# Renumbering the slots of the expert rows, and scattering the second half's rows without copies

## The chip, the cores and the metric

The kernel runs on one core of one Trainium2 chip. The metric is device time of one execution in microseconds, from runs of the kernel with the same inputs. A timed figure is the median of several runs; a profile is taken of one further execution. TensorE's clock has two levels, 1.2 and 2.4 GHz, which the profile gives as a granted clock of 0.50 and 1.00.

## What is computed

Two gated layers on x of 64 sequences, 128 tokens each, width 128, with a context of 77 rows per sequence. Each layer is cross attention, then a feed-forward part, both added to x through a tanh gate:

```python
x = x + tanh(g_xattn[0]) * xattn0(layernorm(x), ctx)      # 8 heads of 64
x = x + tanh(g_ffn[0])   * moe(layernorm(x))              # 16 experts, the best 2 of each token
x = x + tanh(g_xattn[1]) * xattn1(layernorm(x), ctx, ctx) # 16 heads of 8
x = x + tanh(g_ffn[1])   * fp8_gemm(layernorm(x))
```

The change lies in the second line, whose core is

```python
vals, idx = top_k(logits, 2)
w = softmax(vals)
h = relu(x @ W1[e] + b1[e]);  y_e = h @ W2[e] + b2[e]     # 128 -> 256 -> 128
out = sum over the two chosen experts of w * y_e
```

## The kernel before

The kernel has three stages, each a pipeline over blocks of 128 tokens (one sequence) or over expert tiles of 128 rows. All five engines run programs of their own that meet on semaphores.

*Stage A* (`step_a`, 64 blocks, some 0 to 465 us): first cross attention, layer norm, gate logits. VectorE picks the two experts of each token along the way. The normed tokens stay in `XN` ("moe_in").

*Routing* (`route(c)`): the tokens are taken in two halves (c = 0, 1) of 32 blocks. When a half has its picks, TensorE counts and VectorE computes in one chain of instructions, each waiting for the one before (`link`), the slot of every token in a list sorted by expert, each expert's part padded to full tiles of 128. The slots go to `POS[k]`, one column per block and k = 0, 1 for the two picks (line 998). The chain ends with the table of experts per tile (line 1014), for which TensorE waits. Routing 0 runs in the middle of stage A, at 260 to 271 us, routing 1 at its end, at 467 to 478 us.

*Scatter*: GpSimd writes the rows of each block to their slots in a DRAM buffer `xs_dram[c]` by two indirect transfers, one for each pick. For half 0 this happens inside stage A; for half 1 in a loop of its own, right after routing 1, while stage B works on half 0. `scatter` (lines 514 to 525) copies the block's rows and its two columns of slots to small buffers first, waits for those copies, and then issues. A semaphore holds it to two blocks in flight.

*Stage B* (`step_b`, 160 tiles, 80 a half, some 480 to 707 us): each tile is transposed (line 1340), multiplied by W1, gets its bias on VectorE, is transposed again (line 1326), goes through relu on ScalarE, is multiplied by W2 and gets the second bias. SyncE loads four tiles at a time (`load_group`, 20 groups a half, two buffers) and stores four results at a time (`store_group`). Before the first load of a half it waits for all scatters of that half (`scattered(c)`); what stands behind in its queue, stores of the half before among it, waits too. A load also waits until the tiles that were in its buffer are transposed (`xsT_mm`), which puts load g after 4(g - 1) transposes.

*After the scatters* GpSimd waits for all of them, prepares constants of stage C (lines 579 to 595) and gathers results: 48 early gathers during the second half of stage B, each paced by the count of transposes, the rest in stage C. A gather takes its indices straight from `POS[k][:, b:b + 1]` and writes into `XN`.

*Stage C* (`step_c`, 64 blocks with 17 steps of lag, some 707 to 1150 us): the two gathered rows are weighted and added, then second cross attention, the fp8 product and the store.

## Time and profile before

| | |
|---|---|
| median of 3 runs | 1159.11 us (1157.23 to 1159.70) |
| the profiled execution's own time | 1153.63 us |
| its span, first to last instruction | 1151.9 us |
| mean granted clock of TensorE | 0.952 |
| busy in the span | TensorE 1035.9 us, VectorE 814.5, GpSimd 650.7, ScalarE 590.3 |
| stage A with routing 1 | 0 to 479.8 us |
| stage B, half 0 / half 1 | first transposes at 479.8 / 598.8 us |
| last transpose of stage B | 700.2 us |

The profile gives busy time by engine, the span in 40 slices of 28.8 us with the granted clock, then the waits: which engine's instruction stood idle until which other instruction or transfer was done. A wait that is long in total costs nothing where its engine isn't the one that everything waits for. The order of reading is: which engine is busy, in which slices it isn't, what it waits for there, and what that in turn waited for. Lines with an index number are single instructions in order of time.

### The profile page before, as it was taken

Reading aid. Unit: us, or ns where it says so; the run is one execution under the profiler, and the core shown is the slowest. Engines: PE = TensorE matmul, PEld = TensorE weight load, DVE = VectorE, ACT = ScalarE, POOL = GpSimd, SP = SyncE. Lnnn points to the kernel's source line nnn. Section 1 sums busy time; section 2 is a strip of 40 time slices with the busy share of each in tenths; the row PEclk is TensorE's granted clock in tenths of the full one; section 3 lists DMA queues with packets and bytes.
Section 4 is the critical chain, followed back from the end, with each engine's and each line's share of the span. In section 5 each row is a group of like instructions: output and inputs, shape, how many; then the busy total and the mean of one; then the engine's idle time right before and its main releaser. Section 6 shows DMA issues by size and latency. Waiting matters only on the chain. (4 is left out here: it accounts for less than half of the span.)

```text
span 1151.9 us, 40516 instructions
## 1 busy us (share of the span) xinstructions
PE 1035.9 (90%) x13498; PEld 844.1 (73%) x13498; DVE 814.5 (71%) x2572; ACT 590.3 (51%) x1415; POOL 650.7 (56%) x1155
## 2 busy tenths in 40 slices
PE   4999999996999997499949996888999999899993
PEld 3787878774777775288848985666788888788882
DVE  1777777776777775655525555577899999799984
ACT  2666666662666564144515442234556555465554
POOL 1333333232777777566663545447777777577656
PEclk9999999997999999599979998799999999899997
DMA  3412112331334300144424543111111111111101
GB/s 76 90 42 52 42 38 61 91 75 40 92 95 108 98 25 27 55 139 140 134 74 130 144 137 89 30 30 29 32 38 37 32 37 38 30 37 34 33 24 31
DMA packets 106902, 74.39 MB, mean 65 GB/s; under 512 B 21360, under 2 KB 98288, under 8 KB 106736
## 3 DMA queue, kind: packets, MB, share of 16 engines
q1 hardware_dynamic: 98544, 55.40, 18.5%
q0 software_dynamic: 8192, 16.79, 4.9%
q8 instruction: 102, 1.67, 0.6%
q14 instruction: 64, 0.52, 0.2%
HBM read 38.60 MB, written 33.55 MB: 63 GB/s over the span
## 5 line engine op out<-in xcount | busy, mean ns | idle before, releaser
L678 ACT ACTIVATE arena<-PS 77x512 f32<-77x512 f32 (+4 forms) x736 | 303.9, 439 | 424.7 <-PE PS L1194 288.4
L1194 PE MATMUL PS<-arena 128*32 128x128 f32 (+5 forms) x9488 | 452.0, 292 | 36.6 <-DMA logit_bias<-in_bias 12.7
L1194 PEld LDWEIGHTS PS<-arena 128*32 128x32 f32 (+4 forms) x9488 | 352.5, 147 | 114.4 <-ACT arena L678 29.1
L604 POOL DMA_INDIRECT moe_in<-moe_results,slot x128 | 130.5, 1020 | 129.1 <-PE PS L1194 63.0
L1194 PE MATMUL PS<-w,arena 128*128 x960 | 192.4, 319 | 2.2 <-ACT arena L741 1.2
L524 POOL DMA_INDIRECT moe_rows<-arena x128 | 127.5, 996 | 71.8 <-POOL arena L520 50.3
L539 POOL TENSOR_TENSOR arena<-arena,minus_half 128x2 f32<-128x2 f32 (+1 forms) x70 | 47.5, 679 | 187.9 <-DVE arena L852 165.8
L1194 PEld LDWEIGHTS PS<-w,arena 128*128 128x128 f32 x960 | 135.0, 195 | 19.3 <-issue 6.2
L1075 DVE TENSOR_TENSOR arena<-PS,b_rows 128x256 f32<-128x256 f32 x160 | 67.7, 424 | 72.1 <-PE PS L1194 50.1
L1194 PEld LDWEIGHTS PS<-arena,wk_wq 128*128 128x128 f32 x512 | 80.3, 197 | 45.5 <-issue 43.0
L1087 DVE TENSOR_REDUCE arena<-PS 128x8 f32<-128x616 f32 x128 | 96.3, 794 | 18.4 <-PE PS L1194 13.1
L741 ACT ACTIVATE arena<-PS 128x256 f32<-128x256 f32 x160 | 61.3, 384 | 79.8 <-PE PS L1326 67.2
L1194 PE MATMUL PS<-wo,arena 128*128 128x128 f32 x640 | 99.8, 287 | 1.8 <-ACT arena L678 1.2
L1194 PE MATMUL PS<-arena,wk_wq 128*128 128x154 f32 x512 | 97.9, 316 | 1.5 <-ACT arena L678 0.8
L766 ACT ACTIVATE arena<-PS 128x1536 f32<-128x1536 f32 x64 | 93.3, 1458 | 0.0
L1194 PEld LDWEIGHTS PS<-wo,arena 128*128 128x128 f32 x640 | 83.6, 193 | 12.2 <-ACT arena L678 2.9
L546 POOL TENSOR_TENSOR arena<-arena 128x616 f32<-128x616 f32 x64 | 78.1, 1220 | 21.6 <-DVE arena L918 21.5
L889 DVE TENSOR_REDUCE arena<-PS 128x8 f32<-128x616 f32 x64 | 51.1, 799 | 54.5 <-PE PS L1194 54.5
L661 POOL TENSOR_TENSOR arena<-arena,minus_half 128x2 f32<-128x2 f32 (+1 forms) x71 | 51.1, 719 | 60.6 <-DVE arena L1173 60.5
L1148 DVE RECIPROCAL arena<-PS 128x128 f32<-128x128 f32 x64 | 61.2, 956 | 33.7 <-PE PS L1194 20.4
L1068 DVE TENSOR_TENSOR arena<-PS,b_rows 128x128 f32<-128x128 f32 x160 | 45.8, 287 | 47.1 <-PE PS L1194 44.1
L1271 PE MATMUL PS<-ident,arena 128*77 128x128 f32 x512 | 68.8, 277 | 1.2 <-ACT arena L678 0.9
(149 smaller groups left out, 1648.8 us busy)
## 6 DMA issues: line engine op xcount, KB each, us to landing
moe_rows<-zeros SPq DMA_DIRECT2D x64, 160.0 KB, 2.5
arena<-moe_rows SPq DMA_DIRECT2D x40, 256.0 KB
moe_results<-arena SPq DMA_DIRECT2D x40, 256.0 KB
residual<-in_x SPq DMA_DIRECT2D x64, 64.0 KB
w<-in_W SPq DMA_DIRECT2D x32, 128.0 KB
arena<-in_ctxC SPq DMA_DIRECT2D x64, 64.0 KB
out<-arena SPq DMA_DIRECT2D x64, 64.0 KB, 1.6
arena<-in_ctxT SPq DMA_DIRECT2D x32, 77.0 KB
```

The source lines that it names most:

```text
L524: g.indirect_dma_start(out=xs_flat[c][:, :], out_offset=bass.IndirectOffsetOnAxis(ap=si[2 * p + k], axis=0), in_=scat[p], in_offset=None). ...
L546: g.tensor_tensor(pv, pv, rd0[t.par(3)].rearrange("q (h o) -> q h o", o=1).to_broadcast([P, H0, J]), ALU.mult).then_inc(s["P0_made"], 1)
L604: g.indirect_dma_start(out=gathered(b, k), out_offset=None, in_=ys_flat[b // CB][:, :], in_offset=bass.IndirectOffsetOnAxis(ap=POS[k][:, b ...
L661: g.tensor_tensor(rsc[t.par(0)][:, cols], vc[t.par(0)][:, cols], mhalf[:, cols], ALU.pow).then_inc(s["rsc_made"], 1)
L678: A.activation(o, i, ACT.Copy).then_inc(s[done], 1)
L741: A.activation(hT[p], PS[:, 4 + p, 0:EH], ACT.Relu).then_inc(s["hT_cp"], 1)
L766: A.activation(PT1[t.par(6)].rearrange("q (g w) -> q g w", g=NG), PS[:, 4:4 + NG, 0:TAIL], ACT.Exp, scale=DH1 ** -0.5).then_inc(s["exp1"], 1)
L1075: V.tensor_tensor(hb[p], PS[:, 2 + p, 0:EH], b1s[:, bass.ds(e, 1), :].rearrange("q o h -> q (o h)"), ALU.add).then_inc(s["h_made"], 1)
L1087: V.tensor_reduce(mx1[:, 2 * i * KEYS:2 * (i + 1) * KEYS].rearrange("q (g k) -> q g k", g=2)[:, :, 0:GH], PS[:, 2 * i:2 * i + 2, 0:GH * J] ...
L1148: V.reciprocal(rd1, PS[:, 1, 0:P]).then_inc(s["rd1_made"], 1)
L1194: return T.matmul(o, l, r, start=start, stop=stop)
L1271: last = T.transpose(PS[0:J, 2 + h // HB0, (h % HB0) * P:(h % HB0 + 1) * P], P0[p][:, h * J:(h + 1) * J], ident[:, :])
```

## The change

Two things, and what they need.

1. *The slots are renumbered inside each group of four tiles* (512 slots). Row r of tile k in a group had slot 128k + r in the group; now it has 4r + k. VectorE computes this from the old number by five integer instructions in place of the one cast, for each of the two picks and in both routings. Load and store of a group then read and write, for each of 128 partitions, four rows that are contiguous in DRAM (2 KB), where they were four separate rows of 512 B. Which row is in which tile and partition stays the same.

2. *The second half's scatters* take rows straight from `XN` and slots straight from `POS`, as the gathers do, with no copies. The loop is written out over its 32 blocks. Block i of the half (b = 32 + i) waits for 2i transposes of stage B, besides the wait for the block two before it. The first half's scatters still make their copies.

```diff
+        for name in ("slot", "in_tile", "in_group"):
+            rt[name] = ca(CB).bitcast(I32)
@@ load_group and store_group
-                    "(k p) d -> p k d", p=P)).then_inc(s[f"xs_loaded{p}"], 16)
+                    "(p k) d -> p k d", p=P)).then_inc(s[f"xs_loaded{p}"], 16)
...
-                sp.dma_start(ys_flat[c][bass.ds((g - c * NG_B) * (GT * P), GT * P), :].rearrange("(k p) d -> p k d", p=P),
+                sp.dma_start(ys_flat[c][bass.ds((g - c * NG_B) * (GT * P), GT * P), :].rearrange("(p k) d -> p k d", p=P),
@@ GpSimd, after routing 1
-            with pool.Fori(0, CB // 2) as turn:
-                for p in range(2):
-                    scatter(1, turn * 2 + p, p)
+            for b in range(CB, NB):
+
+                p = b % 2
+                pool.wait_ge(s[f"scat_made{p}"], (b - p) * 16)
+                wait_free(pool, s["xsT_mm"], 2 * (b - CB))
+                apart(pool)
+                for k in range(2):
+                    g.indirect_dma_start(out=xs_flat[1][:, :],
+                                         out_offset=bass.IndirectOffsetOnAxis(ap=POS[k][:, b:b + 1], axis=0),
+                                         in_=XN[:, b, :], in_offset=None).then_inc(s[f"scat_made{p}"], 16)
@@ VectorE, route(c), for k in range(2)
-                    link(V.tensor_copy(POS[k][:, lo:lo + CB], rt["m"]), "ro")
+                    link(V.tensor_copy(rt["slot"], rt["m"]), "ro")
+                    link(V.tensor_scalar(rt["in_tile"], rt["slot"], P - 1, 2, ALU.bitwise_and, ALU.logical_shift_left), "ro")
+                    link(V.tensor_scalar(rt["in_group"], rt["slot"], 7, GT - 1, ALU.logical_shift_right, ALU.bitwise_and), "ro")
+                    link(V.tensor_tensor(rt["in_tile"], rt["in_tile"], rt["in_group"], ALU.bitwise_or), "ro")
+                    link(V.tensor_scalar(rt["slot"], rt["slot"], -GT * P, None, ALU.bitwise_and), "ro")
+                    link(V.tensor_tensor(POS[k][:, lo:lo + CB], rt["slot"], rt["in_tile"], ALU.bitwise_or), "ro")
```

## Rows read from the trace of the kernel before

**Rows 1.** The page: busy us by engine, and granted clock in 40 slices.

```profile
PE 1035.9 (90%) x13498; PEld 844.1 (73%) x13498; DVE 814.5 (71%) x2572; ACT 590.3 (51%) x1415; POOL 650.7 (56%) x1155
...
PEclk9999999997999999599979998799999999899997
```

**Rows 2.** Waits from 480 to 700 us: who for whom, us in total, times, longest.

```profile
PE PS L1340 <- DMA arena<-moe_rows: 15.3, 1, 15.3
```

**Rows 3.** Windows of 5 us: length, busy PE, PEld, DVE, ACT, POOL, clock, DMA share, GB/s.

```profile
590.00:595.00 5.00, 0.00 (x0) 0.00 (x0) 0.00 (x0) 0.00 (x0) 3.38 (x6) 0.50 0.12 39
595.00:600.00 5.00, 1.20 (x6) 1.20 (x7) 0.00 (x0) 0.28 (x1) 3.43 (x15) 0.50 0.58 168
600.00:605.00 5.00, 5.00 (x23) 4.33 (x23) 1.72 (x5) 1.55 (x5) 1.35 (x10) 0.60 0.18 56
```

**Rows 4.** TensorE's instructions in time: start, us, engine, line, what, count, [idle before].

```profile
479.75 0.69 PE L1340 MATMUL PS<-ident,arena 128*128 128x128 f32 x2 [0.45 <-DVE bo L1038]
...
577.19 0.27 PE L1340 MATMUL PS<-ident,arena 128*128 128x128 f32 x1
...
582.16 0.27 PE L1340 MATMUL PS<-ident,arena 128*128 128x128 f32 x1
...
598.80 0.48 PE L1340 MATMUL PS<-ident,arena 128*128 128x128 f32 x1 [15.27 <-DMA arena<-moe_rows]
...
605.00 0.27 PE L1340 MATMUL PS<-ident,arena 128*128 128x128 f32 x1
...
606.21 0.27 PE L1340 MATMUL PS<-ident,arena 128*128 128x128 f32 x1
```

**Rows 5.** SyncE's queue in time: loads of groups 19 and 20.

```profile
572.68 0.38 SPq L431 DMA_DIRECT2D arena<-moe_rows  x1
...
595.88 0.37 SPq L431 DMA_DIRECT2D arena<-moe_rows  x1
```

**Rows 6.** Waits of SyncE's queue from 570 to 600 us.

```profile
SPq L57 <- DMA moe_rows<-arena: 20.1, 1, 20.1
```

**Rows 7.** GpSimd in time: one block's scatter, and the end of the last.

```profile
478.49 0.29 POOL L518 COPY arena<-moe_in 128x128 f32 x1 [5.41 <-DVE tile_experts L1014]
...
488.23 0.96 POOL L524 DMA_INDIRECT moe_rows<-arena  x1 [0.30 <-issue]
...
490.51 0.98 POOL L524 DMA_INDIRECT moe_rows<-arena  x1 [0.78 <-POOL arena L520]
491.80 0.95 POOL L524 DMA_INDIRECT moe_rows<-arena  x1 [0.30 <-issue]
...
593.52 0.95 POOL L524 DMA_INDIRECT moe_rows<-arena  x1 [0.30 <-issue]
595.89 1.15 POOL L579 MEMSET arena<- 128x384 f32 x4 [1.42 <-DMA moe_rows<-arena]
```

**Rows 8.** GpSimd in time: two gathers that nothing holds.

```profile
698.85 0.94 POOL L604 DMA_INDIRECT moe_in<-moe_results,slot  x1 [0.30 <-issue]
700.10 0.94 POOL L604 DMA_INDIRECT moe_in<-moe_results,slot  x1 [0.30 <-issue]
```

**Rows 9.** Windows of 90 us, the transposes of line 1340 alone, one per tile.

```profile
490.00:580.00 90.00, 19.36 (x71) 9.89 (x70) 1.00 0.45 137
606.00:696.00 90.00, 19.63 (x72) 10.18 (x72) 1.00 0.49 139
```

**Rows 10.** VectorE in time: the cast, its successor, and an integer mask elsewhere.

```profile
268.98 0.18 DVE L998 CAST slot<-arena 128x32 int32<-128x32 f32 x1
269.19 0.18 DVE L1001 TENSOR_SCALAR arena<-arena 128x32 f32<-128x32 f32 x1
...
480.84 0.23 DVE L1044 TENSOR_SCALAR arena<-arena 128x128 int32<-128x128 int32 x1
```

**Rows 11.** Waits over the whole span: TensorE for the last instruction of a routing.

```profile
PE PS L1194 <- DVE tile_experts L1014: 13.6, 2, 7.0
```

**Rows 12.** The page's DMA issues: KB each, median us from issue to landing.

```profile
moe_rows<-zeros SPq DMA_DIRECT2D x64, 160.0 KB, 2.5
```

## The prediction

> **What bounds the kernel now.** I read the page first. TensorE is busy 90% of the span, no other engine more than 71% [rows 1]. So the kernel is bound by TensorE nearly everywhere, and a change that touches neither its instructions nor its clock can only pay where TensorE stands still. The slices say where: its clock row dips in the 10th slice of 28.8 us (the first routing), the 17th (the second), the 21st (the joint between the two halves of the experts' stage) and the 25th and 26th (the start of the last stage), besides one dip inside the last stage and one at its end [rows 1].
>
> Next the waits in the stretch around the 21st slice. They name one long wait of TensorE, 15.3 us on the transpose of an expert tile, ended by the load of the gathered rows [rows 2]. In the five-microsecond windows TensorE has no instruction from 590 to 595 us, and it comes back at half clock, 0.50 and then 0.60 granted (0.50 is 1.2 GHz, 1.00 is 2.4 GHz) [rows 3]. The single instructions give the size: the last transpose of the first half starts at 582.16, the first of the second half at 598.80, the fourth at 605.00 [rows 4]; in full clock four tiles take 4.97 us or less (577.19 to 582.16, the 76th to the 80th transpose), and two next to each other can be 1.21 apart (605.00, 606.21).
>
> What was late? The queue of SyncE shows it: load 19 goes out at 572.68, the load of group 20 only at 595.88 [rows 5]. SyncE stood 20.1 us on the scatters of the second half [rows 6]. The scatters come from GpSimd: a block takes 3.57 us (488.23 to 491.80 from second transfer to second transfer), of which the three copies and the wait behind them fill the time from 489.2, where the second transfer's issue ends, to 490.51; the last transfer is issued at 593.52 and has landed 1.42 us after its issue ends, when GpSimd goes on at 595.89 [rows 7]. So 32 blocks at 3.57 us are 114 us, while TensorE needs 102.4 us for the 80 tiles of the first half (479.75 to 582.16, [rows 4]). GpSimd loses the race, and TensorE pays for the difference.
>
> **The change part by part.** The sum is made against the profiled execution: span 1151.9 us, its own time 1153.63, 1.7 us outside the span. The three timed runs have their median at 1159.11, 0.5% above it. The difference that I work out should not depend on that; I put it on the median.
>
> *1. Scatters without copies.* What remains per block are two indirect transfers. Before, one of them costs 0.98 + 0.30 us and the next 0.96 [rows 7], and with a second pause of 0.30 that is 2.54 us. Gathers in the same kernel, which take source and indices straight from the big tiles as the scatters now do, follow each other at 1.25 us when nothing holds them (698.85, 700.10), 2.5 us a block [rows 8]. From the other side: if the 0.78 us pause that now stands between index copy and first transfer stays in spite of the missing copies, a block is 0.98 + 0.30 + 0.96 + 0.78 = 3.02 us. I take 2.54, since the gathers do just this. The saving lies on GpSimd and reaches the end only through the stall.
>
> *2. The pacing.* Block i of the second half now waits for 2i transposes of the first half. Queued behind that wait on GpSimd are only the later scatters, then four memsets and small set-up of the last stage, which wait for the scatters before as well. TensorE moves through two tiles in 2 x 90/71 = 2.54 us [rows 9], just the rate of GpSimd itself. The last block waits for 62 transposes. The 62nd is about 18 tiles before the last at 582.16, at some 559.3; with the 2.15 us of part 3 at 561.5, its transfers end at 564 and have landed at some 565.5. The load of group 20 in SyncE's order goes out after 76 transposes, four tiles after load 19: at 572.68 + 4.97 = 577.65, or 579.8 with the shift [rows 4, 5]. So the scatters are ready 14 us ahead. Even at 3.02 us a block they end at 480.6 + 96.6 + 1.4 = 578.7, still ahead. The wait of 20.1 us on SyncE goes, and what is late next is nothing: load 20 needs 2.9 us to be used (595.88 to 598.80, [rows 4, 5]) and tile 80 is due 1.21 us after the 80th transpose, at 583.4, so 5.7 us after the load's issue.
> The stall is worth 598.80 - 582.16 - 1.21 = 15.4 us. The half clock behind it goes too, because it follows only from TensorE's rest: 605.00 - 598.80 = 6.20 us for three tiles that otherwise take 3.63, so 2.6 us. Together -18.0 us. Stores 17 to 19 and the first gathers hang on tiles 80 to 88 and move along with them; the early gathers are paced by tiles and keep their place in TensorE's order.
>
> *3. The renumbering on VectorE.* In each of the two routings one cast into the slot table becomes a cast and five integer instructions, for two picks: ten more, each waiting for the one before. The cast on the same 128x32 shape takes 0.18 us and the next starts 0.21 after its start (268.98, 269.19) [rows 10]. With the waits, 0.21 to 0.22 each, ten are 2.15 us; an integer mask on 128x128 takes 0.23 us [rows 10], with the same 0.03 pause at most 2.6. All of it lies on the path: TensorE waits for the last instruction of this chain 13.6 us in the two routings, the longer time 7.0 [rows 11], with nothing else to do. Twice 2.15 are +4.3 us (bounds 4.2 to 5.2). [...]
> The Trainium skill, VectorE: DVE Perf Modes, section "The TRN2 errata — SBUF-src ops pay a fixed extra latency per instruction", has a table by which such an instruction is (58 + 32)/0.96 GHz = 94 ns, an estimate from that page; with it this part would be 2.6 us instead of 4.3 and the whole difference 1.7 us better. A note under the table puts the fixed term nearer 150 cycles, which is 190 ns and what the 0.18 us of the trace supports.
>
> *4. Loads and stores with four contiguous rows of a partition.* A load or store of 256 KB moves in runs of 2 KB instead of 512 B. In the experts' stage no load but the one at the joint holds up TensorE [rows 2], so a quicker landing is hidden by the double buffer and worth 0. It could help only by leaving the memory queues freer. TensorE's quickest pace is 1.21 us a tile, its mean 90/71 = 1.27 in the first half and 90/72 = 1.25 in the second, where GpSimd issues transfers without copies [rows 9]. If the first half comes to the second's pace, that is 80 x 0.02 = 1.4 us; if every hesitation went in both, 160 x 0.05 = 8 us. I take 0, since neither row ties them to these transfers, and keep -1.4 in the range.
>
> Sum: -18.0 + 4.3 + 0 = -13.7 us. On the profiled execution 1139.9, on the median 1159.1 - 13.7 = 1145.4.
>
> **The rivals.** *Part of the stall stays.* The scatters have 97.8 us, from 480.6 (478.49 before, [rows 7], and the shift) to 579.8 less 1.4 for landing, that is 3.06 us a block. Load 20 has 2.8 us to spare (5.7 - 2.9); beyond, each 0.1 us a block costs 3.2 us of stall. At 3.2 to 3.4 us, for instance because the waits and the no-op ahead of each block take longer than the copies' wait did, 2 to 8 us would stay: about 1151. For it speaks that a pause of 0.78 us stands there before; against it that the gathers, with the same no-op, pause 0.30 [rows 8].
> *No gain from the scatters.* If a transfer straight from the big tile took what copy and transfer took, 3.57 us a block, the stall would stay and the ten instructions twice be paid: 1163. Against it stand the gathers again.
> *Loads that land late.* A load has 5.7 us until TensorE needs it and takes 2.9 now. If runs of 2 KB, each filling one partition, went slower (fewer, longer pieces spread worse over the 16 engines), then from 5.7 us each microsecond costs 40 us over 40 groups. It eats the gain at 5.7 + 13.7/40 = 6.0 us a load; at 6.3 the kernel would be at 1145 + 24 = 1169. Against it: clearing the row buffer moves 160 KB in runs of 2.5 KB and lands in 2.5 us [rows 12], and the DMA engines are under half loaded in the experts' stage [rows 9].
> *The hesitations go as well.* With the queues freer, up to 8 us more: near 1139.
>
> **How the numbers follow.** My forecast has 0.82, part of the stall 0.07, no gain 0.03, late loads 0.03, the hesitations 0.05. The range must hold 8 in 10. The forecast itself spreads: from -15.1 (pace of the second half) to -12.8 (5.2 us of added instructions), and its base lies between the profiled execution (1153.6) and the highest run (1159.7). That gives 1138.5 to 1147; taken out to the partial stall above and to some of the hesitations below: 1137 to 1151. A measurement of this kernel can tell 0.2% (2.3 us) from no change. Faster by more than that: the forecast, the hesitations and nearly all of the partial stall, 0.93. Within: 0.02. Slower: no gain, late loads, 0.05.
>
> **What the changed profile would show.** Right: no wait of TensorE on the load at the joint, no window without TensorE instructions between the halves, clock 1.00 through both; SyncE's wait on scatters gone; GpSimd's scatters of the second half in pairs with no copies, waiting for TensorE's transpose, done some 15 us before the first half ends; the waits for the routing's last instruction 2.1 to 2.2 us longer each. Wrong: GpSimd never waiting for a transpose and TensorE still idle at the joint (rivals 1, 2); TensorE waiting for loads inside a half (rival 3); tiles under 1.25 us apart on average (rival 4). The prediction fails as a whole if the last stage turns out to depend on when its set-up on GpSimd is ready, or on anything else the shift of 14 us moves.

## The result, and the profile of the changed kernel

The changed kernel takes **1168.21 us** (median of 7 runs, 1165.41 to 1172.35) against 1159.11 of the kernel before (7 runs, 1153.93 to 1159.70). The ratio is 1.0094, 95% interval 1.0077 to 1.0112: slower by some 11 us in the mean (9.1 between the medians) where 13.7 us less were forecast. The profiled execution took 1169.6 us, its span is 1167.8, 15.9 us more than before; that is more than the timed runs give because the profiled execution before, 1153.63 us, lies 5.5 below its median and this one 1.4 above.

Of the page, the lines that answer to [rows 1]:

```profile
PE 1040.7 (89%) x13496; PEld 845.7 (72%) x13498; DVE 818.6 (70%) x2592; ACT 589.5 (50%) x1415; POOL 633.0 (54%) x1059
...
PEclk9999999997999998599999997799999999999996
```

The dip at the joint, in the 21st slice before, is gone. The single transposes say the same (start, us, engine, line): the last of the first half and the first of the second, against 582.16 and 598.80 in [rows 4].

```profile
610.37 0.27 PE L1354 MATMUL PS<-ident,arena 128*128 128x128 f32 x1
611.57 0.27 PE L1354 MATMUL PS<-ident,arena 128*128 128x128 f32 x1
```

They stand 1.20 us apart, and in the waits from 570 to 620 us neither TensorE nor SyncE waits for a load or a scatter any more. But the 80th transpose is 28 us later than before. Windows of the transposes alone, one per tile (length, busy PE, PEld, clock, DMA share, GB/s), the first as in [rows 9]:

```profile
490.00:580.00 90.00, 14.89 (x53) 7.91 (x53) 0.94 0.33 112
606.00:696.00 90.00, 19.62 (x72) 10.19 (x72) 1.00 0.42 136
```

Before, 71 tiles lay in the first window; now 53 do, while the second half keeps its 72. The granted clock of the first window is 0.94 where it was 1.00. The span adds up so, with the start of tile 1, 80, 81 and 160 as marks:

| stretch | before | after | difference |
|---|---|---|---|
| start to tile 1 (both routings) | 479.75 | 484.47 | +4.7 |
| tile 1 to 80 | 102.41 | 125.90 | **+23.5** |
| tile 80 to 81, the joint | 16.64 | 1.20 | **-15.4** |
| tile 81 to 160 | 101.38 | 99.02 | -2.4 |
| tile 160 to the end | 451.7 | 457.2 | +5.5 |

So the stall went, as forecast, and a larger loss came up in the stretch just ahead of it. What is it made of? TensorE is busy 106.2 us between tile 1 and tile 80 where it was busy 99.9, with a granted clock of 0.93 and 0.96: 6.3 us are instructions that took longer, the other 17 are idle time. Every engine raises a semaphore when an instruction that another engine waits for is done; I call that its increment. The waits from 484 to 612 us have entries whose releaser is "remote": an instruction waited for an increment, and no instruction in the profile ended just before it came.

```profile
DVE arena L1089 <- remote: 11.9, 5, 3.4
POOL moe_rows L579 <- remote: 9.7, 5, 2.0
ACT arena L750 <- remote: 8.8, 3, 3.5
DVE arena L1082 <- remote: 6.7, 4, 2.4
ACT arena L687 <- remote: 4.3, 4, 1.1
```

One of these stalls in order of time, on four engines:

```profile
511.53 0.96 POOL L579 DMA_INDIRECT moe_rows<-moe_in,slot  x1 [0.30 <-issue]
...
512.58 0.38 PE L1340 MATMUL PS<-ident,arena 128*128 128x128 f32 x2
...
513.06 0.96 POOL L579 DMA_INDIRECT moe_rows<-moe_in,slot  x1 [0.57 <-issue]
...
513.78 0.38 PE L1340 MATMUL PS<-ident,arena 128*128 128x128 f32 x2
...
514.32 0.96 POOL L579 DMA_INDIRECT moe_rows<-moe_in,slot  x1 [0.30 <-issue]
...
516.09 0.38 ACT L750 ACTIVATE arena<-PS 128x256 f32<-128x256 f32 x1 [3.48 <-remote]
516.31 0.42 DVE L1089 TENSOR_TENSOR arena<-PS,b_rows 128x256 f32<-128x256 f32 x1 [1.20 <-remote]
...
516.60 0.68 PE L1208 MATMUL PS<-w,arena 128*128 x4 [1.89 <-ACT arena L750]
```

ScalarE's relu (L750) needs the two transposes of L1340 of its tile, and an older product of TensorE that comes ahead of them in TensorE's order. The relus and transposes of the stage come in the same order, and the one at 516.09 belongs to the transposes of 512.58, through at 512.96. ScalarE has been idle since 512.61 and still starts 3.1 us after them. TensorE goes on 0.1 us after ScalarE's result is there (516.47 to 516.60). So TensorE's own increment reached ScalarE late, and TensorE then waited for the work that this had held up. From the 9th tile to the 80th 17 distances between tiles are above 1.6 us, together 26.9 us above the undisturbed 1.21. This stall comes behind four indirect transfers issued one after the other (here 510.27 to 514.32).

The traces also record when each increment came. Set against the end of the last instruction before it that makes this increment (which can only put it too small), the lateness of TensorE's increments follows GpSimd's indirect transfers (e3 and e9 are runs that come below):

| trace, stretch in us | indirect transfers in it | TensorE's increments recorded | over 0.2 us late | latest, us |
|---|---|---|---|---|
| before, 0 to 255 | 0 | 358 | 0 | |
| before, 485 to 575 | 49 | 219 | 66 | 1.1 |
| changed, 0 to 255 | 0 | 358 | 0 | |
| changed, 485 to 575 | 52 | 170 | 78 | 2.5 |
| e3, 485 to 575 | 61 | 35 | 23 | 19.9 |
| e3, 575 to 645 | 0 | 227 | 0 | |
| e9 (the changed kernel on another chip), 485 to 575 | 59 | 287 | 0 | |

No increment of ScalarE, VectorE or GpSimd is over 0.2 us late in any trace up to 1050 us (behind that the matching of increments to instructions fails, on all chips). SyncE's loads and stores run in all of these stretches, so it isn't transfers as such.

### The profile page after: what moved, and what is told of

Same layout as the page of the kernel before. It is cut to its first block and busy times, and to the rows that moved or that the text cites. A ratio compares the mean times of both kernels' runs of the same rounds, so it can differ in the third digit from the quotient of the medians.

```text
span 1167.8 us, 40261 instructions
## 1 busy us (share of the span) xinstructions
PE 1040.7 (89%) x13496; PEld 845.7 (72%) x13498; DVE 818.6 (70%) x2592; ACT 589.5 (50%) x1415; POOL 633.0 (54%) x1059
## 5 line engine op out<-in xcount | busy, mean ns | idle before, releaser
L1208 PE MATMUL PS<-arena 128*32 128x128 f32 (+5 forms) x9488 | 452.8, 292 | 40.7 <-DMA logit_bias<-in_bias 12.3
L1208 PE MATMUL PS<-w,arena 128*128 x960 | 195.7, 322 | 16.4 <-issue 7.8
L1208 PEld LDWEIGHTS PS<-w,arena 128*128 128x128 f32 x960 | 137.5, 198 | 36.3 <-issue 25.1
L750 ACT ACTIVATE arena<-PS 128x256 f32<-128x256 f32 x160 | 61.3, 384 | 95.9 <-PE PS L1340 76.3
L579 POOL DMA_INDIRECT moe_rows<-moe_in,slot x64 | 61.2, 957 | 55.0 <-issue 24.6
L1162 DVE RECIPROCAL arena<-PS 128x128 f32<-128x128 f32 x64 | 61.2, 957 | 35.8 <-PE PS L1208 21.7
L526 POOL DMA_INDIRECT moe_rows<-arena x64 | 65.6, 1025 | 35.2 <-POOL arena L522 25.4
```

The lines of the kernel that those rows point to most:

```text
L526: g.indirect_dma_start(out=xs_flat[c][:, :], out_offset=bass.IndirectOffsetOnAxis(ap=si[2 * p + k], axis=0), in_=scat[p], in_offset=None). ...
L579: g.indirect_dma_start(out=xs_flat[1][:, :], out_offset=bass.IndirectOffsetOnAxis(ap=POS[k][:, b:b + 1], axis=0), in_=XN[:, b, :], in_offs ...
L750: A.activation(hT[p], PS[:, 4 + p, 0:EH], ACT.Relu).then_inc(s["hT_cp"], 1)
L1162: V.reciprocal(rd1, PS[:, 1, 0:P]).then_inc(s["rd1_made"], 1)
L1208: return T.matmul(o, l, r, start=start, stop=stop)
```

## The experiments

Eighteen runs in five groups; the kernels of a group share their runs of the kernel before. The groups fell on chips of two kinds, and this decides how they are read. So the kernel before comes first, as each group measured it:

```
group        chip   kernel before, us   tile, 9th to 80th (mean)
(the result)  ?     1159.1              1.281
e1 to e4      0     1152.7              1.280 (e1), 1.261 (e4)
e5 to e8      7     1130.9              1.209 (e5), 1.208 (e8)
e9 to e12     7     1129.1              1.209 (e12)
e13 to e16    7     1131.4              1.209 (e14)
e17, e18      1     1152.9              1.278 (e18)
```

(The kernels named at the right leave the first half's tiles as they were.) I call chips 0 and 1 the first kind and chip 7 the second. No chip was seen in both conditions, chip 7 three times in the same; whether it is the chip itself or something else that held on it during these runs isn't shown. The result above has every mark of the first kind: 1159 us, 1.28 us a tile, and waits on "remote".

### Which part of the change costs

The first four runs set the two parts apart. My first theory was that the loads' runs of 2 KB get in the way of the scatters; its rival, that the scatters without copies themselves do it, because they are closer together.

*e1: the renumbering alone.* The loops of the kernel before, with the diff of `load_group`, `store_group` and `route`, and no change on GpSimd:

```diff
-                    link(V.tensor_copy(POS[k][:, lo:lo + CB], rt["m"]), "ro")
+                    link(V.tensor_copy(rt["slot"], rt["m"]), "ro")
...
+                    link(V.tensor_tensor(POS[k][:, lo:lo + CB], rt["slot"], rt["in_tile"], ALU.bitwise_or), "ro")
```

> The kernel before with the renumbering and the 2 KB runs of loads and stores alone; the second half's scatters keep their copies and their loop, and wait for no transposes. In the changed kernel the first half of the experts' stage takes 125.9 us from first to last transpose, before 102.4, with 17 gaps of over 1.6 us between transposes. Theory A (the 2 KB runs collide with scatters, whatever these look like): the first half takes 115 to 126 us here too, the joint's stall shrinks to what is left, kernel at 1165 to 1175. Theory B (the scatters without copies, or their pacing, hold up TensorE): first half as before, 102 to 104 us, the stall of 15 us stays, and only the ten added instructions per routing count: 1162 to 1166.

Measured: 1158.05 us, ratio 1.0040 (1.0023 to 1.0057). The first 80 tiles take 103.8 us, with 4 distances above 1.6 us as before. Runs of 2 KB disturb nothing and give nothing that these figures show; what is left is the routing, forecast at +4.3 us = 0.37%.

*e2: the scatters alone*, written out, without copies, paced, with the old numbering (the diff of GpSimd only).

> The kernel before with the second half's scatters direct, written out and paced, but with the old slot numbers and 512 B runs. Theory A (2 KB runs are needed for the collision): first half near 100 to 103 us, no stall at the joint, 1139 to 1145. Theory B (direct, paced scatters alone do it): first half at 120 to 126 us with some 17 long gaps, about 1162 to 1166.

Measured: 1157.25 us, ratio 1.0030 (1.0013 to 1.0048). The first 80 tiles take 123.9 us, with 22 distances above 1.6; the joint is 1.21 us. That is the changed kernel's picture without the renumbering.

*e3: the changed kernel without the pacing.*

```diff
                 pool.wait_ge(s[f"scat_made{p}"], (b - p) * 16)
-                wait_free(pool, s["xsT_mm"], 2 * (b - CB))
                 apart(pool)
```

> The changed kernel without the wait for 2i transposes. If the pacing is at fault (GpSimd and TensorE in lockstep), the long gaps go, the scatters run at 2.5 us a block and end near 565 us, first half near 102 us, kernel near 1145. If the scatters' rate or form is at fault, the gaps stay while scatters run (some 80 us) and first half takes 118 us or more, kernel 1160 to 1170.

Measured: 1209.05 us, ratio 1.0489 (1.0452 to 1.0526). So the pacing isn't what costs; it keeps a much larger loss down. Windows of the transposes of e3, the same 90 us as above:

```profile
490.00:580.00 90.00, 4.31 (x12) 2.46 (x13) 0.55 0.17 57
```

Twelve tiles in 90 us. The granted clock is 0.55 there, so part of the loss is that TensorE, idle most of the time, also works slower in between (0.69 us for two transposes that take 0.38 at full clock). Its rows show the mechanism bare. First TensorE's second transposition of a tile (of h), then ScalarE's relu, which waits for it, then the last of the scatters:

```profile
494.58 0.38 PE L1339 MATMUL PS<-ident,arena 128*128 128x128 f32 x2
495.79 0.38 PE L1339 MATMUL PS<-ident,arena 128*128 128x128 f32 x2
502.12 0.69 PE L1339 MATMUL PS<-ident,arena 128*128 128x128 f32 x2 [1.05 <-issue]
516.15 0.69 PE L1339 MATMUL PS<-ident,arena 128*128 128x128 f32 x2 [3.23 <-DVE arena L1088]
535.68 0.69 PE L1339 MATMUL PS<-ident,arena 128*128 128x128 f32 x2 [3.87 <-issue]
```

```profile
499.25 0.38 ACT L749 ACTIVATE arena<-PS 128x256 f32<-128x256 f32 x1 [2.60 <-remote]
511.21 0.38 ACT L749 ACTIVATE arena<-PS 128x256 f32<-128x256 f32 x1 [9.51 <-remote]
530.11 0.38 ACT L749 ACTIVATE arena<-PS 128x256 f32<-128x256 f32 x1 [12.32 <-remote]
554.61 0.38 ACT L749 ACTIVATE arena<-PS 128x256 f32<-128x256 f32 x1 [15.82 <-remote]
572.15 0.38 ACT L749 ACTIVATE arena<-PS 128x256 f32<-128x256 f32 x1 [8.17 <-remote]
```

```profile
565.41 0.96 POOL L578 DMA_INDIRECT moe_rows<-moe_in,slot  x1 [0.30 <-DMA moe_rows<-moe_in,slot]
```

The two lists belong together row by row: they are the 5th to 9th transposes and the 5th to 9th relus of the stage. From the end of one to the start of the other it is 4.3, 15.0, 27.3, 37.8 and 35.8 us, and no more than 0.04 us again from the 11th on (574.37); the last late one comes at 572.3, 7 us after the last scatter is issued. The increments come in order and late, as if they stood in a line that moves on while GpSimd issues a transfer every 1.26 us. Between the last scatter and the first gather GpSimd issues no transfer, and this chip runs its tiles at 1.21 us, with SyncE's loads and stores going on:

```profile
578.00:645.00 67.00, 14.99 (x55) 7.79 (x55) 1.00 0.34 111
```

VectorE's and ScalarE's increments to TensorE show no such delay: TensorE takes up the relu of 554.61, over at 554.99, with a matmul at 555.12, and the transpose of 535.68 starts 0.06 us after VectorE's addition ends. Nor are the DMA engines full: they are 17% busy in the 90 us window.

*e4: the scatters of the kernel before, with their copies, only written out.*

```diff
-            with pool.Fori(0, CB // 2) as turn:
-                for p in range(2):
-                    scatter(1, turn * 2 + p, p)
+            for b in range(CB):
+                scatter(1, b, b % 2)
```

> The kernel before with the second half's 32 scatters written out instead of a loop, copies, slot numbers and runs as before. If written-out code on GpSimd is what holds up TensorE (instructions that have to be fetched), the first half takes 110 us or more, with long gaps. If not, all is as before: 102 us, stall of 15 us, 1155 to 1160.

Measured: 1153.16 us, ratio 1.0007 (0.9989 to 1.0026); 80 tiles in 101.1 us, a joint of 18.0. The written-out code is not it. What is left is that transfers without copies either follow each other too closely (theory R, for rate) or harm by their form (theory F). Form alone can't be it: the scatters of the kernel before have their copies, and 66 of 219 increments are late beside them.

### Rate or form: a group that fell on the other kind of chip

*e5: the direct form at the old rate.* As e4, but source and list are those of the direct scatters, and the three copies are made for nothing:

```diff
+                g.tensor_copy(scat[p], XN[:, bass.ds(b, 1), :].rearrange("q o d -> q (o d)")).then_inc(s["idx_made"], 1)
...
+                                         out_offset=bass.IndirectOffsetOnAxis(ap=POS[k][:, b:b + 1], axis=0),
+                                         in_=XN[:, b, :], in_offset=None).then_inc(s[f"scat_made{p}"], 16)
```

> The second half's scatters are written out, unpaced, and read XN and POS directly, but the three copies that they no longer need are still made ahead of each pair, so a block of two transfers takes GpSimd about 3.57 us as in the kernel before. Theory R (what harms is how closely the indirect transfers follow each other): the first 80 tiles take 100 to 104 us as in the kernel before, the stall of about 15 us between the halves stays, and the time is 0.998 to 1.003 of the kernel before. Theory F (what harms is what the transfer reads: its rows straight from the wide array XN, its list straight from POS): the first 80 tiles have the gaps of the kernel after, 115 to 125 us, part of it taken from the stall, and the time is 1.003 or more of the kernel before.

*e6: direct, old numbering, one transfer each six fifths of a tile*; *e7: the same mean rate in pairs.* Both are shown against e2:

```diff
-                wait_free(pool, s["xsT_mm"], 2 * (b - CB))
-                apart(pool)
                 for k in range(2):
+                    wait_free(pool, s["xsT_mm"], 6 * (2 * (b - CB) + k) // 5)
+                    apart(pool)
```

```diff
-                wait_free(pool, s["xsT_mm"], 2 * (b - CB))
+                wait_free(pool, s["xsT_mm"], 12 * (b - CB) // 5)
```

> Scatters without copies, old numbering, each single transfer i of 64 waits for tile 6i/5 instead of each pair for tile 2 per block: one transfer each 1.53 us at an undisturbed 1.275 us a tile. Theory R with room for a transfer in about 1.5 to 1.6 us: the first 80 tiles take 103 to 108 us (123.9 with the pacing of one transfer a tile), the stall between the halves is under 5 us instead of 15, and the time is 0.987 to 0.993 of the kernel before (205 to 210 us from the first to the 160th tile, against 220.4). If the room is nearer 1.7 us a transfer, the first 80 tiles take 64 x 1.7 = 109 us or more and the time is 0.993 to 0.998. Theory F (the direct form itself harms): 1.002 or more, with gaps of about 2 us as in the kernel after.

> As the run with single transfers at 6/5 of a tile, but both transfers of a block go out together, each pair waiting for tile 12/5 per block: the same mean rate in bursts of two. Theory R by the mean rate: the first 80 tiles within 1 us of the run with single transfers, the same time within 0.2%. Rival theory R2 (the distance of two neighbours counts, below about 1.3 us a transfer delays TensorE's increments whatever follows): a gap of 0.5 to 1 us after each of the 32 pairs, the first 80 tiles 10 us or more longer than with single transfers, the time about 0.5 to 1% above it.

*e8: the kernel before with its early gathers closer together*, one a tile instead of two in three tiles.

```diff
-                pool.wait_ge(s["xsT_mm"], NT + 8 + 3 * i // 2)
+                pool.wait_ge(s["xsT_mm"], NT + 8 + i)
```

> The kernel before with one edit in its second half: the 48 early gathers, also indirect transfers of GpSimd, wait for one tile each instead of one and a half, so they are issued about every 1.27 us instead of 1.9 us. Theory R (any close indirect transfers of GpSimd delay TensorE's increments): over these 48 tiles the tile time goes from 1.26 to about 1.5 to 1.6 us, the second 80 tiles take 112 to 118 us instead of 101.4, the first 80 tiles are untouched, and the time is 1.006 to 1.014 of the kernel before. Rival (only the scatters, which write to HBM, do it): the second 80 tiles take 100 to 102.5 us, the time is within 0.2% of the kernel before.

Measured: e5 1131.76 us, 1.0001 (0.9984 to 1.0017); e6 1108.23 us, **0.9786** (0.9765 to 0.9807); e7 1107.75 us, **0.9776** (0.9757 to 0.9795); e8 1131.40 us, 1.0002 (0.9986 to 1.0017). By these figures theory R fell with e8: for 48 gathers, 1.34 us apart in the mean and some 1.26,

```profile
644.99 0.94 POOL L604 DMA_INDIRECT moe_in<-moe_results,slot  x1 [0.30 <-DMA moe_in<-moe_results,slot]
646.25 0.94 POOL L604 DMA_INDIRECT moe_in<-moe_results,slot  x1 [0.31 <-PE PS L1340]
```

tiles went on at 1.21 us. And e6 and e7 gained more than the stall is worth in [rows 4]. But the kernel before itself had changed: 1131 us, and not one wait on "remote" in any trace of this group. Either the chip decides (theory X) or the transfers' distance of six fifths (S); the next group was made to tell these apart, with kernels already known on chip 0.

### The same kernels on the second kind of chip

*e9* is the changed kernel itself, *e10* is e3's kernel, *e11* e6's and *e12* e8's, unaltered.

> The changed kernel itself once more. Theory X (the late increments of TensorE are a condition of the chip that the run is on, present where the kernel before takes 1152 to 1160 us and its undisturbed tile 1.28 us, absent where it takes 1131 us and its tile 1.21 us): beside a kernel before of about 1131 us the first 80 tiles take 96 to 99 us, no increment is later than 0.1 us, and the time is 0.980 to 0.984 of the kernel before (that of the paced pairs, 0.978, and 4.3 us of added routing). Beside a kernel before of 1152 us or more it is 1.007 to 1.012 again. Rival theory S (the chip doesn't matter, what matters is that the transfers come one tile apart instead of six fifths): 1.005 or more beside either.

> The changed kernel with the second half's scatters unpaced, once more. Theory X: beside a kernel before of about 1131 us no increment is later than 0.1 us, all 64 transfers are out within about 83 us, the first 80 tiles take 96 to 100 us, and the time is within 0.3% of the changed kernel's. Beside a kernel before of 1152 us or more: the first 80 tiles take about 170 us, the time is 1.045 to 1.053 of it. Rival S: the latter beside either.

> The direct scatters one at a time, each six fifths of a tile after the last, once more. Theory X beside a kernel before of about 1131 us: 0.977 to 0.981 of it again. Beside a kernel before of 1152 us or more, with the room for a transfer of 1.5 to 1.6 us there: the first 80 tiles take 103 to 110 us, the time is 0.987 to 0.996 of the kernel before; if the backlog builds up all the same, 1.00 or more. Rival S: 0.977 to 0.981 beside either.

> The kernel before with its 48 early gathers one tile apart instead of one and a half, once more. Theory X beside a kernel before of about 1131 us: within 0.2% of it again. Beside a kernel before of 1152 us or more: the second 80 tiles take 110 to 120 us instead of 101.4, the time is 1.006 to 1.016 of it. Rival S, and a rival by which only transfers that write to HBM delay anything: within 0.2% beside either.

Measured: e9 1112.67 us, **0.9854** (0.9825 to 0.9882); e10 1115.86 us, 0.9866 (0.9832 to 0.9900); e11 1108.25 us, 0.9810 (0.9783 to 0.9837); e12 1130.79 us, 1.0010 (0.9995 to 1.0025). The same program as e3, which lost 4.9% on chip 0, gains 1.3% on chip 7. Windows of the transposes of e10, and then its rows with the same GpSimd issues of one transfer per 1.26 us:

```profile
490.00:580.00 90.00, 20.21 (x73) 10.50 (x73) 0.98 0.46 146
```

```profile
533.09 0.96 POOL L578 DMA_INDIRECT moe_rows<-moe_in,slot  x1 [0.31 <-DMA moe_rows<-moe_in,slot]
...
533.92 0.38 PE L1339 MATMUL PS<-ident,arena 128*128 128x128 f32 x2
534.34 0.38 ACT L749 ACTIVATE arena<-PS 128x256 f32<-128x256 f32 x1 [0.39 <-PE PS L1339]
534.36 0.96 POOL L578 DMA_INDIRECT moe_rows<-moe_in,slot  x1 [0.30 <-issue]
```

73 tiles instead of 12, and 0.04 us from TensorE's end to ScalarE's start instead of up to 37.8, also at the densest run of transfers. Theory X holds, with what was said above of "chip", and S fell. Over the 160 tiles no increment from this transpose to this relu is later than 0.2 us in any trace of chip 7.

### The first kind of chip again

The next two groups are about what stayed open on the first kind: rate, gathers, form, kind of transfer. *e13*, *e14* and *e15* are the kernels of e6, e8 and e5; *e16*, with the old numbering and unpaced, has ordinary transfers in place of the indirect ones. They leave out the list of slots, so the rows don't reach the slots of their experts and the output is not the reference's:

```diff
-                    g.indirect_dma_start(out=xs_flat[1][:, :],
-                                         out_offset=bass.IndirectOffsetOnAxis(ap=POS[k][:, b:b + 1], axis=0),
-                                         in_=XN[:, b, :], in_offset=None).then_inc(s[f"scat_made{p}"], 16)
+                    i = 2 * (b - CB) + k
+                    g.dma_start(out=xs_flat[1][i * P:(i + 1) * P, :], in_=XN[:, b, :]).then_inc(s[f"scat_made{p}"], 16)
```

> Direct scatters, one at a time, each six fifths of a tile after the last. On a chip of the first kind (the kernel before at 1152 us or more): by the theory that the delay grows with the rate, with room for a transfer in 1.5 to 1.6 us, the first 80 tiles take 103 to 110 us and the time is 0.987 to 0.996 of the kernel before; by its rival, that the direct form itself does it, 120 us or more and 1.00 or more. On a chip of the second kind (1129 to 1131 us): 0.977 to 0.983 again.

> The kernel before with the 48 early gathers one tile apart. On a chip of the first kind: if any close indirect transfers of GpSimd delay TensorE's increments, the second 80 tiles take 110 to 120 us instead of 101.4 and the time is 1.006 to 1.016 of the kernel before; if only the scatters do, 100 to 102.5 us and within 0.2%. On a chip of the second kind: within 0.2% again.

> Direct scatters with the three copies still made ahead of each pair (two transfers in 3.57 us). On a chip of the first kind: by the rate, the first 80 tiles take 100 to 104 us and the time is 0.998 to 1.003 of the kernel before; by the form, 115 us or more and 1.003 or more. On a chip of the second kind: 0.998 to 1.002 again.

> The second half's 64 scatters are ordinary transfers of GpSimd, unpaced, each to 128 rows in order instead of to rows from a list: the tokens of this half don't reach their slots, and the output is not the reference's. The same bytes in the same number of transfers, but no list. On a chip of the first kind: if it takes the list (GpSimd working out each row's address), the first 80 tiles take 96 to 103 us and the time is 0.980 to 0.992 of the kernel before; if any of GpSimd's transfers in close order do it, 120 us or more and 1.00 or more. On a chip of the second kind: 0.976 to 0.985 either way, with the stall between the halves gone.

They fell on chip 7 once more and so leave that question open: e13 1108.70 us, 0.9787 (0.9763 to 0.9811); e14 1130.76 us, 1.0004 (0.9987 to 1.0022); e15 1130.69 us, 0.9987 (0.9974 to 1.0000); e16 1107.28 us, 0.9774 (0.9756 to 0.9793), nothing later than 0.2 us in any of them. They give the stall of this kind of chip, though. e15, whose scatters are as slow as before:

```profile
PE PS L1349 <- DMA arena<-moe_rows: 20.3, 1, 20.3
```

20.3 us, where [rows 2] have 15.3: TensorE is through its 80 tiles in 97.3 us instead of 102.4, GpSimd's 114 us stay, and the difference is the stall.

*e17: the changed kernel with e6's pacing*, and *e18: e8's kernel*, both on a chip of the first kind.

> The changed kernel with its second half's scatters one at a time, each six fifths of a tile after the last. On a chip of the first kind: with room for a transfer in 1.5 to 1.6 us the first 80 tiles take 103 to 110 us (125.9 in the changed kernel) and the time is 0.990 to 0.999 of the kernel before; if it is the direct form whatever the rate, 1.005 or more. On a chip of the second kind: the renumbering costs 4 to 5 us of routing beside the same kernel with the old numbering (0.979 to 0.981), so 0.982 to 0.986; if the larger loads gave something back, 0.978 to 0.981.

> The kernel before with the 48 early gathers one tile apart. On a chip of the first kind: if any close indirect transfers of GpSimd delay TensorE's increments, the second 80 tiles take 110 to 120 us instead of 101.4 and the time is 1.006 to 1.016 of the kernel before; if only the scatters do, 100 to 102.5 us and within 0.2%. On a chip of the second kind: within 0.2% again.

Measured: e17 1153.68 us, 1.0019 (0.9999 to 1.0040); e18 1169.45 us, **1.0138** (1.0092 to 1.0184). Windows of e18's transposes, and under them those of e8, the same program on chip 7, for the 70 us from 606:

```profile
606.00:676.00 70.00, 12.37 (x45) 6.46 (x45) 0.98 0.43 121
```

```profile
606.00:676.00 70.00, 15.65 (x58) 8.23 (x58) 1.00 0.57 156
```

So gathers, which read from DRAM, do it as well as scatters, which write to it: the second 80 tiles of e18 take 123.6 us instead of 101.4, with 19 distances above 1.6 us from the ninth tile of the half on instead of 5, while its first half is untouched (102.6). In e17 the first 80 tiles take 113.6 us, with 14 such distances instead of 17. This is a gain of 12.3 us on the changed kernel by nothing but a pacing one fifth wider, and still 11 us behind the kernel before:

```
kernel (chip kind 1)        us per transfer   mean tile   distances > 1.6 us
e3, unpaced                       1.26            2.25          7 (74 us in all)
e18, gathers, one a tile          1.63            1.63         15 (20 us)
the changed kernel, e2            1.60, 1.57      1.60, 1.57   17 (27), 22 (25)
e17, 6/5 of a tile                1.72            1.43         14 (16)
the kernel before, scatters       1.78            1.28          4 (2)
```

(Us per transfer: for the paced ones mean tile times tiles per transfer, for the unpaced and the kernel before from issue to issue, 3.57/2 by [rows 7]. Mean tile: 9th to 80th; for e18, distances too, the 48 tiles of its gathers, 609.96 to 688.23. In brackets what these distances are above 1.21 us.) The three kernels with one transfer a tile are one step of this table: for them the first two columns are the same number by the way they are paced. From step to step, unpaced, one a tile, 6/5 of a tile, the kernel before, the mean tile falls with the rate. No rate among these is free of loss; what my expectation for e17 said, room for a transfer in 1.5 to 1.6 us and 103 to 110 us for the half, was too hopeful by 3.6 us at least.

## Why the prediction was wrong

**What bounds the kernel, and the stall: right.** GpSimd's 32 blocks against TensorE's 80 tiles was the cause of the wait at the joint, and with shorter blocks it went to 1.20 us, on both kinds of chip.

**Part 1, scatters without copies: right in size.** The last transfers of the changed kernel:

```profile
585.47 0.96 POOL L579 DMA_INDIRECT moe_rows<-moe_in,slot  x1 [0.30 <-issue]
586.73 0.96 POOL L579 DMA_INDIRECT moe_rows<-moe_in,slot  x1 [0.30 <-issue]
589.58 0.96 POOL L579 DMA_INDIRECT moe_rows<-moe_in,slot  x1 [1.89 <-PE PS L1354]
```

1.26 us from one to the next, 2.52 a block, 2.54 forecast. The rival of no gain from the scatters had nothing behind it.

**Part 2, the pacing: this step failed.** It set TensorE's pace as given, "TensorE moves through two tiles in 2 x 90/71 = 2.54 us [rows 9], just the rate of GpSimd itself", and asked only whether GpSimd keeps up. The saving "lies on GpSimd and reaches the end only through the stall": that GpSimd's transfers could slow the engine they are hidden behind was nowhere priced. They did: two tiles took 3.19 us. And because the transfers are paced by tiles, and the tiles slowed by transfers, the two settled at a common pace of one transfer a tile at 1.60 us. -18.0 was forecast for stall and half clock; -15.4 at the joint and -2.4 in the second half came, 17.8 in all, and +23.5 with them, a term that the sum did not have.

**Part 3, the renumbering: right.** A cast and five integer instructions stand where one cast stood (not five in place of it, as the section on the change has it). The chain in the first routing, against [rows 10]:

```profile
269.72 0.18 DVE L1007 CAST arena<-arena 128x32 int32<-128x32 f32 x1
269.94 0.18 DVE L1008 TENSOR_SCALAR arena<-arena 128x32 int32<-128x32 int32 x1
...
271.04 0.18 DVE L1015 TENSOR_SCALAR arena<-arena 128x32 f32<-128x32 f32 x1
```

From the cast to what follows it is 1.32 us, five instructions of 0.22 more than the 0.21 before. The wait of TensorE for the routings, 13.6 us in [rows 11], is

```profile
PE PS L1208 <- DVE tile_experts L1028: 18.0, 2, 9.2
```

+4.4 us against +4.3, and the longer of the two 2.2 longer. e1 has the same 18.0 us, and its ratio puts the whole of it at 4.6 us (0.40% of 1152.66, 2.7 to 6.6). The estimate of 2.6 us in the prediction, from the table in the Trainium skill, VectorE: DVE Perf Modes, section "The TRN2 errata — SBUF-src ops pay a fixed extra latency per instruction", is not what the rows show: each of these instructions takes 0.18 us, as before. The sum has nothing for the half clock behind the second routing; the granted clock is 1.00 again 8.2 us after tile 1 in the kernel before and 9.9 us after it in the changed one.

**Part 4, the runs of 2 KB: right at 0** (e1: 103.8 us for the first half, 102.4 before). But this part held the clue. It noted that tiles came every 1.27 us on average where 1.21 was possible, 8 us in all, and took nothing for it "since neither row ties them to these transfers". The trace has the tie, though not in those rows. Between 485 and 575 us, beside GpSimd's scatters, 66 of 219 increments of TensorE come more than 0.2 us late, 1.1 at most; in e9 none of 287 does. They stand under TensorE's own name in the waits there, so the stage has no "remote". But the last stage, where GpSimd gathers, has it for VectorE, in the waits of the kernel before over its whole span:

```profile
DVE arena L1148 <- remote: 13.2, 8, 1.7
```

It is 22.2 us in all; the changed kernel has 76.5, and none of the traces of chip 7 has any. With no transfer of GpSimd beside them the tiles of e3, on the same kind of chip, came every 1.21 us. So the hesitations were this same delay at a low rate, a price per transfer that grows with the rate, and not a reserve that a change might free. The rival that the hesitations go too had the sign the wrong way round on this kind of chip.

**The other rivals.** Part of the stall stays, and loads that land late, didn't occur: no load is waited for within a half. The time came out slower by a mechanism that was on no list, and the 0.93 for faster was worth no more than the list of rivals. The condition named at the end, that the last stage might move, can't be settled: it is 5.5 us longer in the two traces, but between 444.9 and 457.2 us in the traces of all kernels on chips of the first kind, though none of the edits touches it. Late increments of TensorE are there as well on the first kind (44 of 255 recorded between 760 and 900 us in the kernel before), and none in e9, where that stage takes 434.9 us.

**On the second kind of chip the sum would have stood.** e9 measures 1112.67 - 1129.06 = -16.4 us (-13.3 to -19.8); forecast -13.7. By the parts there, with e15, which has the stall, as the kernel before: 596.25 - 574.60 = 21.65 us at the joint become 1.20, -20.4; +4.4 of routing (18.0 us of waits against 13.6 there too); -2.4 in the second half (98.1 to 95.7): -18.4. The term that the sum had too small is the stall, 15.4 against 20.4, because TensorE is at 1.21 us a tile there. So it wasn't the arithmetic that failed but one unlisted interaction, which two of the three chips showed. That the sum comes out on the third is no credit to the forecast, which didn't know of the condition.

**How the lateness comes about stays open.** Shown is: only increments from TensorE are late; they come in order; they are late only where GpSimd issues indirect transfers and just behind, whether these write to DRAM or read from it, with copies or without; the lateness grows with their rate; the same program has none of it on chip 7. Whether ordinary transfers of GpSimd do it as well wasn't seen on the first kind (e16 fell on the second), nor whether the direct form adds something at the old rate (e5, e15), nor e6 with the old numbering. A rival that no run tests: the recording itself. In the same stretches, and only on the first kind, records of increments are missing, those of ScalarE and VectorE too (of the 640 that these two make in stage B the trace of the kernel before has 492, that of e8 636; ahead of the first indirect transfer, at 280 us, both traces have 920 of these two). So what makes TensorE's increments late may also hold up the records, or the writing of records may be part of the cause; every time here is from an execution that has a span and a clock, so one without a recording wasn't seen. The Trainium skill, Perfetto Trace Analysis, section "Tensor Engine Instruction (MATMUL, LD_WEIGHTS)", says that a matmul's end in the profile is an estimate, and that the increment goes out only when PSUM has acknowledged the last byte, and must then propagate. If so, the 37.8 us may lie in either step, and no row here separates them. The Trainium skill, SBUF — State Buffer, section "SBUF: two separate sides", says that a DMA cannot be slowed by a compute op or the reverse, and that TensorE and ScalarE never wait on anyone there. TensorE's instructions themselves were hardly slower (a tile's transpose takes 280 ns in the mean in the changed kernel, 278 in e9), which agrees. What was late is the handover behind them, by up to 37.8 us, and that is no access to SBUF.

**A kernel that beats both** exists on the second kind: direct scatters with the old numbering, 6/5 or 12/5 of a tile apart, at 0.978 to 0.981 (e6, e7, e11, e13) against 0.9854 of the changed kernel in e9. On the first kind, e17 ties with the kernel before; taking its 4.4 us of renumbering off would give 0.998, an estimate that was not run.

## What to carry to other kernels

Before more work is hidden behind the busiest engine, price what it does to that engine: compare its mean pace with its quickest in stretches with more and with less of that work, and read unexplained releasers as a price that grows with the rate. A queue paced by the progress of the engine it disturbs doesn't free that engine, it settles into a common slower pace; spacing it wider gave back 12 us of 23 here. And measure a change on more than one chip: the same two programs stood at 1.0094 and at 0.9854. The quickest way to see such a thing in one trace is to compare a stretch without the suspected transfers, as in the table of increments above.

## What the runs showed of the hardware

- Indirect transfers of GpSimd delay TensorE's semaphore increments on some chips, and only TensorE's (in the kernel before none of 358 up to 255 us, where there are no such transfers, and 66 of 219 between 485 and 575 us): by 3.1 us behind four transfers close together in the changed kernel, by up to 37.8 us with 64 in a row at 1.26 us each (e3). On chip 7 the same 64 delay none by over 0.2 us (e10).
- Two kinds of chip: the kernel before takes 1152.7 and 1152.9 us on chips 0 and 1, and 1129.1 to 1131.4 us on chip 7, with 1.28 against 1.21 us a tile, and 445 to 457 against 435 to 438 us from the 160th tile to the end. The granted clock isn't the reason for the tiles: it is 1.00 from 606 to 676 us in e8 and in the kernel before. Nor are the tiles slower by themselves: on chip 0 they come every 1.21 us too while GpSimd issues nothing (e3, 578 to 645 us).
- Loads in runs of 2 KB and of 512 B are worth the same here, with the DMA engines 42 to 45% busy (e1, windows of 490 to 580 and 606 to 696 us).
